# ScalarE's table loads moved to the end of the stages, and the masked attention's fill made by ScalarE

## The chip, the cores and the metric

The kernel runs on one core of a Trainium2 chip. A core has a matrix engine (TensorE, PE), a vector engine (VectorE, DVE), an activation engine (ScalarE, ACT), a general engine (GpSimd, POOL) and a queue for transfers (SyncE, SP). They run side by side, each in its own order, and wait for each other by semaphores. SBUF is the memory they work in, PSUM holds TensorE's results. The metric is device time in microseconds (us), lower is better. ScalarE looks its functions up in a table that holds one set of functions at a time; another set has to be loaded with an instruction of its own (ACT_TABLE_LOAD).

## The reference

Sixteen sequences of 128 tokens with 128 features pass through four layers, each with a cross attention and a feed-forward part, each part on a normalised copy of x and added to x through a gate:

```python
x = x + tanh(g_xattn[0]) * L0_xattn(layernorm(x), ctx, ...)     # correlation attention
x = x + tanh(g_ffn[0])   * L0_ffn(layernorm(x), ...)            # one of 8 experts
x = x + tanh(g_xattn[1]) * L1_xattn(layernorm(x), ctx, ...)     # 16 heads
x = x + tanh(g_ffn[1])   * L1_ffn(layernorm(x), ...)            # experts that choose tokens, silu
x = x + tanh(g_xattn[2]) * L2_xattn(layernorm(x), ctx, ...)     # 16 heads
x = x + tanh(g_ffn[2])   * L2_ffn(layernorm(x), ...)            # modulated MLP, gelu
x = x + tanh(g_xattn[3]) * L3_xattn(layernorm(x), ctx, mask, ...)
x = x + tanh(g_ffn[3])   * L3_ffn(layernorm(x), ...)            # small attention, 8 experts, gelu

def L3_xattn(q, k, v, mask, gamma, beta):                       # the masked attention
    logits = einsum('bsd,btd->bst', q, k) / sqrt(128)
    logits = where(mask == 0, -9e15, logits)
    x = einsum('bst,btd->bsd', softmax(logits), v)
    return layernorm_without_affine(x) * gamma + beta
```

All is float32, the mask is int32.

## The kernel before, in words

The whole model is one program. x stays in SBUF as X (128 tokens on the partitions, 16 x 128 columns), its normalised copy is XN, the transposed copy XNT. Each stage is one or several blocks. In a block every engine has its own list of instructions, and at its end all engines meet at a barrier. The order on each engine is the order in which the code is written; no scheduler changes it.

Stages in turn: input norm (L147), correlation attention (L197), experts 0, attention 1, experts 1 (L1350), attention 2, modulated MLP (L1407), masked attention (L1640), block attention (L1803), experts 3 (L2129).

`norm_pass` (L1372) is a block of its own that stands behind five of them: correlation, experts 0, experts 1, modulated MLP and masked attention. The stage has left the mean and variance of each token in `moments`. ScalarE loads the table set LOG_EXP (it has Ln, Exp and Copy), makes one over the square root of the variance out of Ln (L1384) and Exp (L1386), VectorE normalises 16 sequences (L1395), TensorE transposes them (L1403), and ScalarE copies the transposes to XNT (L1389). The experts of layers 1 and 3 go through `expert_quads`, whose ScalarE part (L1275) computes Silu or Gelu (L1285); the modulated MLP uses a tanh Gelu (L1600). Those functions need other table sets than LOG_EXP. The last block (L2149) normalises once more, with a table load of its own (L2152), Ln and Exp, ScalarE's scaling (L2159) and VectorE's sums (L2175 to L2187). LOG_EXP is also loaded at the start of the attentions (L886), of the masked attention (L1713) and of the block attention (L1924).

The masked attention works in four quarters q of four sequences (tiles of 128 x 512). GpSimd makes of the mask the tile hidden_key (1 where the mask is 0, L1673), fill (hidden_key times -9e15, L1676) and open_key (1 - hidden_key, L1677), with two buffers for the last two; behind q = 1 it adds the affine's second row to X, the residual base, in four operations (L1683), for which `scaled` (VectorE, L1790) must be there. TensorE makes the scores of all quarters (L1691), then for each quarter transposes the probabilities (L1699) and multiplies them with the context (L1707). VectorE's `softmax_rows(q)` scales and masks the scores (L1751), adds the fill (L1753), takes the maximum (L1754) and subtracts it (L1755, `shifted`); `output(q)` sums the probabilities (L1760), takes the reciprocal (L1761), scales the product (L1763) and takes its moments (L1765, L1768, `varied`); `add(q)` normalises it and adds it to X (L1777 to L1783), for which `based` must be there. VectorE's order is softmax 0, 1, output 0, softmax 2, output 1, softmax 3, add 0, output 2, add 1, output 3, add 2, add 3. ScalarE's order for each quarter is the exponential (L1718, `exped`), the copy of the transpose (L1722, `kept`), Ln and Exp for the output's norm (L1725, L1727). The functions that the diff touches:

## Time and profile before

| | |
|---|---|
| time before, median of 3 runs | 1493.91 us (1493.3 to 1495.25) |
| profiled execution | 1494.78 us, of it 1493.0 us in the span of the trace |
| TensorE busy | 1282.6 us, 86% |
| VectorE busy | 877.8 us, 59% |
| ScalarE busy | 711.9 us, 48% |
| GpSimd busy | 277.8 us, 19% |
| TensorE's granted clock, mean | 0.924 of full speed |
| the masked attention's block | 990.7 to 1037.4 us |

Times in the trace count from the start of the span. An instruction is busy from its start to its end; idle time of an engine is put down to what ended it. Where an engine is "released by PEq", "ACTq" or "issue", no work that the profile shows released it: it stood at a barrier or took up instructions. A granted clock of 1.00 is 2.4 GHz, of 0.50 it is 1.2 GHz.

### The profile page before, as it was taken

Reading aid. Unit: us, or ns where it says so; the run is one execution under the profiler, and the core shown is the slowest. Engines: PE = TensorE matmul, PEld = TensorE weight load, DVE = VectorE, ACT = ScalarE, POOL = GpSimd, SP = SyncE. Lnnn points to the kernel's source line nnn. Section 1 sums busy time; section 2 is a strip of 40 time slices with the busy share of each in tenths; the row PEclk is TensorE's granted clock in tenths of the full one; section 3 lists DMA queues with packets and bytes.
Section 4 is the critical chain, followed back from the end, with each engine's and each line's share of the span. In section 5 each row is a group of like instructions: output and inputs, shape, how many; then the busy total and the mean of one; then the engine's idle time right before and its main releaser. Section 6 shows DMA issues by size and latency. Waiting matters only on the chain. (4 is left out here: it accounts for less than half of the span.)

```text
span 1493.0 us, 26211 instructions
## 1 busy us (share of the span) xinstructions
PE 1282.6 (86%) x8587; PEld 958.4 (64%) x8587; DVE 877.8 (59%) x2280; ACT 711.9 (48%) x1529; POOL 277.8 (19%) x382
## 2 busy tenths in 40 slices
PE   6768489989987899779999979963999978999995
PEld 5742256666665487568888859852677764666664
DVE  4538788888873454556676643448687742222225
ACT  4323487777772302246666643432455533333333
POOL 1010032222231000023333330041443420000000
PEclk9869799999997999879999989965999978999998
DMA  9000000000000000000000022020000000000000
GB/s 349 2 1 0 1 1 1 2 1 2 2 1 1 1 1 0 1 1 2 2 2 2 2 59 70 1 113 1 1 2 0 0 1 0 0 1 1 0 1 29
DMA packets 6426, 24.48 MB, mean 16 GB/s; under 512 B 797, under 2 KB 1311, under 8 KB 5418
## 3 DMA queue, kind: packets, MB, share of 16 engines
q1 hardware_dynamic: 6314, 23.03, 4.5%
q8 instruction: 65, 1.06, 0.3%
q14 instruction: 47, 0.39, 0.1%
HBM read 21.98 MB, written 1.05 MB: 15 GB/s over the span
## 5 line engine op out<-in xcount | busy, mean ns | idle before, releaser
L1305 DVE SCALAR_TENSOR_TENSOR XN<-bank,gate,XN 128x128 f32<-128x128 f32 x256 | 89.9, 351 | 224.7 <-PE bank L1269 222.1
L1285 ACT ACTIVATE e_hidden<-bank,small 128x512 f32<-128x512 f32 x152 | 104.4, 687 | 214.8 <-PE bank L1257 214.7
L745 POOL TENSOR_TENSOR a_pn<-a_probs,a_rec 128x512 f32<-128x512 f32 x128 | 133.0, 1039 | 308.6 <-DVE a_rec L995 234.5
L1269 PEld LDWEIGHTS bank<-attention_weights,e_hidden 128*128 128x128 f32 x1024 | 119.2, 192 | 14.8 <-issue 14.8
L1009 DVE TENSOR_REDUCE a_mx<-bank 128x4 f32<-128x512 f32 x128 | 87.1, 681 | 70.2 <-PE bank L807 70.2
L1257 PE MATMUL bank<-XNT,attention_weights 128*128 128x512 f32 x256 | 121.2, 606 | 1.3 <-PEq L541 1.3
L1269 PE MATMUL bank<-attention_weights,e_hidden 128*128 128x128 f32 x1024 | 119.3, 275 | 0.0
L931 ACT ACTIVATE a_pT<-bank 128x512 f32<-128x512 f32 x128 | 76.1, 594 | 89.2 <-PE bank L842 89.0
L833 PE MATMUL bank<-attention_weights,a_cv 128*128 128x512 f32 x128 | 70.8, 635 | 27.3 <-issue 25.8
L1017 DVE TENSOR_TENSOR a_shifted<-bank,a_mx 128x512 f32<-128x512 f32 x128 | 88.3, 690 | 3.5
L990 DVE TENSOR_REDUCE a_total<-a_probs 128x4 f32<-128x512 f32 x128 | 86.5, 676 | 1.3 <-ACT a_probs L947 1.3
L1900 PEld LDWEIGHTS bank<-blk_va,blk_pT 128*128 128x128 f32 x512 | 64.3, 193 | 33.8 <-issue 21.8
L842 PEld LDWEIGHTS bank<-consts,a_pn 128*128 128x128 f32 x512 | 60.3, 141 | 38.0 <-issue 33.3
L947 ACT ACTIVATE a_probs<-a_shifted 128x512 f32<-128x512 f32 x128 | 80.0, 625 | 9.4 <-DVE a_shifted L1017 9.4
L1848 POOL TENSOR_TENSOR blk_kD<-blk_kT,consts 128x512 f32<-128x512 f32 x64 | 64.5, 1040 | 86.9 <-ACT blk_va L1947 86.9
L1257 PEld LDWEIGHTS bank<-XNT,attention_weights 128*128 128x128 f32 x256 | 40.8, 189 | 60.0 <-ACT e_hidden L1285 43.2
L842 PE MATMUL bank<-consts,a_pn 128*128 128x128 f32 x512 | 78.7, 276 | 0.8 <-ACT a_pT L931 0.7
L807 PE MATMUL bank<-a_kT,a_qT 64*128 64x128 f32 x1024 | 71.5, 279 | 0.6 <-DVE a_shifted L1017 0.6
L774 PE MATMUL bank<-a_pT,a_va 128*64 128x128 f32 x1024 | 70.0, 279 | 0.0
L807 PEld LDWEIGHTS bank<-a_kT,a_qT 64*128 64x128 f32 x1024 | 65.6, 189 | 6.9 <-issue 6.0
L1882 PE MATMUL bank<-blk_kD,blk_qT 128*128 128x512 f32 x128 | 67.9, 615 | 1.8 <-POOL blk_kD L1848 1.8
L821 PE MATMUL bank<-attention_weights,a_oT 128*128 128x128 f32 x512 | 65.7, 281 | 1.5 <-ACT a_oT L899 1.4
(351 smaller groups left out, 2584.9 us busy)
## 6 DMA issues: line engine op xcount, KB each, us to landing
attention_weights<-in_a SPq DMA_DIRECT2D x2, 2048.0 KB, 11.9
mod_ring<-in_mod_weights SPq DMA_DIRECT2D x4, 576.0 KB
ctx_both<-in_ctx SPq DMA_DIRECT2D x1, 2048.0 KB, 9.8
attention_weights<-in_up SPq DMA_DIRECT2D x1, 2048.0 KB, 7.9
attention_weights<-in_down SPq DMA_DIRECT2D x1, 2048.0 KB, 12.4
down<-in_down SPq DMA_DIRECT2D x1, 1536.0 KB, 18.3
down<-in_mod_weights SPq DMA_DIRECT2D x2, 576.0 KB
X<-in_x SPq DMA_DIRECT2D x4, 256.0 KB, 4.2
```

The costliest lines, as they stand in the source:

```text
L745: pool.tensor_tensor(pn[:, p, :].rearrange("p (h s) -> p h s", h=4), probs[:, p, :].rearrange("p (h s) -> p h s", h=4), rec[:, p, :].unsqu ...
L807: last = pe.matmul(score_bank[a][:, j * 128:(j + 1) * 128], qT[halves[a], p, at_pair:at_pair + 128], kT[halves[a], p, at_pair:at_pair + 12 ...
L842: last = pe.transpose(turn_bank[i.slot(turns)][:, j * 128:(j + 1) * 128], pn[:, p, j * 128:(j + 1) * 128], k.ident)
L931: act.activation(pT[:, i.slot(4), :], turn_bank[i.slot(turns)][:, :], ACT.Copy).then_inc(p_kept, 1)
L947: act.activation(probs[:, p, :], shifted[:, p, :], ACT.Exp, scale=W ** -0.5).then_inc(exped, 1)
L990: dve.tensor_reduce(total[:, p, :], probs[:, p, :].rearrange("p (h s) -> p h s", h=4), AX.X, ALU.add).then_inc(totalled, 1)
L1009: dve.tensor_reduce(mx[:, i.slot(2), :], score_bank[i.slot(2)][:, :].rearrange("p (h s) -> p h s", h=4), AX.X, ALU.max).then_inc(maxed, 1)
L1017: dve.tensor_tensor(shifted[:, p, :].rearrange("p (h s) -> p h s", h=4), score_bank[p][:, :].rearrange("p (h s) -> p h s", h=4), mx[:, p, ...
L1257: pe.matmul(bank[0:rows, :], up(g, f), col(k.XNT, q, 512), start=True, stop=True).then_inc(up_done, 1)
L1269: last = pe.matmul(down_bank[j][:, 0:width], layer[0:rows, f, j * 128:(j + 1) * 128], down(g, f), start=f == 0, stop=f == NB - 1)
L1285: act.activation(hidden[0:rows, p, f, :], up_bank_of(i, f)[0:rows, :], function, bias=up_bias(g, f)).then_inc(hidden_ready, 1)
L1305: dve.scalar_tensor_tensor(out=total, in0=down_bank[j][:, e * D:(e + 1) * D], scalar=gate_column(k, 4 * q + j, g * per_group + e), in1=tot ...
```

## The change

Five things change, all on ScalarE and GpSimd:
- the load of LOG_EXP at the head of `norm_pass`, of the last block, of the attentions, of the masked attention and of the block attention is taken out;
- it is added at the end of ScalarE's part of `expert_quads` (experts 1 and 3), behind the modulated MLP's last Gelu, and at the start of the correlation attention;
- in the masked attention hidden_key has two buffers, and `fill` is made by ScalarE (Copy with scale -9e15) instead of GpSimd: fills 0 and 1 ahead of all else, fill q + 2 behind the exponential of quarter q and ahead of the copy of its transpose;
- GpSimd adds the residual base behind all four masks instead of behind the second;
- VectorE's `softmax_rows` waits for `opened` and the new semaphore `filled`.

```diff
--- before.py
+++ after.py
@@ -272,6 +272,7 @@
 
             @block.scalar
             def _(act):
+                act.preload_act_table_set(LOG_EXP)
                 def body(at):
                     b = at(0)
                     if b.alive:
@@ -883,7 +884,6 @@
 
         @block.scalar
         def _(act):
-            act.preload_act_table_set(LOG_EXP)
 
             def square(i):
                 await_count(act, qk_projected, i.number + 1)
@@ -1286,6 +1286,7 @@
                                        bias=up_bias(g, f)).then_inc(hidden_ready, 1)
                 finish.scalar(act, batch_at(at))
             sweep(act, 4 * groups, groups, finish.depth * pace + FINISH, body)
+            act.preload_act_table_set(LOG_EXP)
 
         @block.vector
         def _(dve):
@@ -1380,7 +1381,6 @@
 
         @block.scalar
         def _(act):
-            act.preload_act_table_set(LOG_EXP)
             act.activation(moments[:, :, 1], moments[:, :, 1], ACT.Ln, bias=k.eps5[:, 0:1]).then_inc(logged, 1)
             act.wait_ge(logged, 1)
             act.activation(moments[:, :, 1], moments[:, :, 1], ACT.Exp, scale=-0.5).then_inc(rstd, 1)
@@ -1608,6 +1608,7 @@
                         keep_w2(n + 2)
                     if n + 1 < B:
                         gelu(n + 1)
+                act.preload_act_table_set(LOG_EXP)
 
             @block.vector
             def _(dve):
@@ -1645,11 +1646,12 @@
     with ExitStack() as ctx:
         sem = lambda what: nc.alloc_semaphore(f"single_{what}")
         sb = lambda what, shape, dt=F32: ctx.enter_context(nc.sbuf_tensor(f"single_{what}", shape, dt))
-        hidden_key, open_key, fill = sb("hidden_key", [128, 512]), sb("open_key", [128, 2, 512]), sb("fill", [128, 2, 512])
+        hidden_key, open_key, fill = sb("hidden_key", [128, 2, 512]), sb("open_key", [128, 2, 512]), sb("fill", [128, 2, 512])
         logits, probs, pT = sb("logits", [128, 2, 512]), sb("probs", [128, 2, 512]), sb("pT", [128, 2, 512])
         mx, rec = sb("mx", [128, 2, 4]), sb("rec", [128, 2, 4])
         o, stats, x_stats = sb("o", [128, 2, 512]), sb("stats", [128, 4, 6]), sb("x_stats", [128, B, 6])
         spread, moments = sb("spread", [128, 2, 4, 2]), sb("moments", [128, B, 2])
+        filled = sem("filled")
         marked, opened, scaled, based = sem("marked"), sem("opened"), sem("scaled"), sem("based")
         summed, x_summed, updated = sem("summed"), sem("x_summed"), sem("updated")
         scored, chain, shifted, exped = sem("scored"), sem("chain"), sem("shifted"), sem("exped")
@@ -1666,22 +1668,20 @@
             def _(pool):
                 pool.wait_ge(k.loaded["mask_ik1"], 16)
                 for q in range(4):
-                    if q:
-                        pool.wait_ge(opened, 2 * q)
                     if q >= 2:
+                        pool.wait_ge(opened, q - 1)
+                        pool.wait_ge(filled, q - 1)
                         pool.wait_ge(shifted, q - 1)
-                    pool.tensor_scalar(hidden_key[:, :], k.mask_ik1[:, q * 512:(q + 1) * 512], 0.0, None,
+                    pool.tensor_scalar(hidden_key[:, q % 2, :], k.mask_ik1[:, q * 512:(q + 1) * 512], 0.0, None,
                                        ALU.is_equal).then_inc(marked, 1)
                     pool.wait_ge(marked, q + 1)
-                    pool.tensor_scalar(fill[:, q % 2, :], hidden_key[:, :], NEG, None, ALU.mult).then_inc(opened, 1)
-                    pool.tensor_scalar(open_key[:, q % 2, :], hidden_key[:, :], -1.0, 1.0, ALU.mult,
+                    pool.tensor_scalar(open_key[:, q % 2, :], hidden_key[:, q % 2, :], -1.0, 1.0, ALU.mult,
                                        ALU.add).then_inc(opened, 1)
-                    if q == 1:
-                        pool.wait_ge(scaled, 1)
-                        for n in range(4):
-                            x = k.X[:, n * 512:(n + 1) * 512].rearrange("p (b d) -> p b d", b=4)
-                            pool.tensor_tensor(x, x, k.affine3(1).unsqueeze(1).to_broadcast([128, 4, D]),
-                                               ALU.add).then_inc(based, 1)
+                pool.wait_ge(scaled, 1)
+                for n in range(4):
+                    x = k.X[:, n * 512:(n + 1) * 512].rearrange("p (b d) -> p b d", b=4)
+                    pool.tensor_tensor(x, x, k.affine3(1).unsqueeze(1).to_broadcast([128, 4, D]),
+                                       ALU.add).then_inc(based, 1)
 
             @block.tensor
             def _(pe):
@@ -1710,12 +1710,21 @@
 
             @block.scalar
             def _(act):
-                act.preload_act_table_set(LOG_EXP)
+                def fill_hidden(q):
+                    act.wait_ge(marked, q + 1)
+                    if q >= 2:
+                        act.wait_ge(shifted, q - 1)
+                    act.activation(fill[:, q % 2, :], hidden_key[:, q % 2, :], ACT.Copy, scale=NEG).then_inc(filled, 1)
+
+                fill_hidden(0)
+                fill_hidden(1)
                 for q in range(4):
                     act.wait_ge(shifted, q + 1)
                     if q >= 2:
                         act.wait_ge(turned, q - 1)
                     act.activation(probs[:, q % 2, :], logits[:, q % 2, :], ACT.Exp).then_inc(exped, 1)
+                    if q + 2 < 4:
+                        fill_hidden(q + 2)
                     act.wait_ge(turned, q + 1)
                     if q >= 2:
                         act.wait_ge(weighted, q - 1)
@@ -1745,7 +1754,8 @@
                 def softmax_rows(q):
                     p, l = q % 2, logits[:, q % 2, :]
                     dve.wait_ge(scored, q + 1)
-                    dve.wait_ge(opened, 2 * q + 2)
+                    dve.wait_ge(opened, q + 1)
+                    dve.wait_ge(filled, q + 1)
                     if q >= 2:
                         dve.wait_ge(exped, q - 1)
                     link(dve.scalar_tensor_tensor(out=l, in0=k.ps[q][:, :], scalar=float(D) ** -0.5,
@@ -1921,7 +1931,6 @@
 
         @block.scalar
         def _(act):
-            act.preload_act_table_set(LOG_EXP)
 
             def body(at):
                 i = at(EXP)
@@ -2149,7 +2158,6 @@
         with nc.Block(no_gpsimd_drain=True) as block:
             @block.scalar
             def _(act):
-                act.preload_act_table_set(LOG_EXP)
                 v = moments[:, :, 1]
                 act.activation(v, v, ACT.Ln, bias=k.eps5[:, 1:2]).then_inc(logged, 1)
                 act.wait_ge(logged, 1)
```

How this stands on the engines. ScalarE at the end of the modulated MLP, the pass behind it and the head of the masked attention, the difference of before (-) and now (+); mod_u is the Gelu's output:

```order
 L1592 ACTIVATE mod_w<-bank 128x512
 L1600 ACTIVATE mod_u<-bank,mod_column_bias 128x128 x8
+L1611 ACT_TABLE_LOAD
 L1519 UNCONDITIONAL_BRANCH
-L1381 UNCONDITIONAL_BRANCH
-L1383 ACT_TABLE_LOAD
+L1382 UNCONDITIONAL_BRANCH
 L1384 ACTIVATE mod_moments<-mod_moments,eps 128x16
 L1386 ACTIVATE mod_moments<-mod_moments 128x16
 L1389 ACTIVATE XNT<-bank 128x512 x4
```

The load has moved from behind the barrier to ahead of it (the branches mark the ends and starts of blocks).

ScalarE in the masked attention's first two quarters now (before, it was L1713's load, then L1718, L1722, L1725, L1727 of each quarter in turn); single_probs is the exponential, single_pT the kept transpose:

```order
L1717 ACTIVATE single_fill<-single_hidden_key 128x512 x2
L1725 ACTIVATE single_probs<-single_logits 128x512
L1717 ACTIVATE single_fill<-single_hidden_key 128x512
L1731 ACTIVATE single_pT<-bank 128x512
L1734 ACTIVATE single_spread<-single_spread,eps 128x4
L1736 ACTIVATE single_spread<-single_spread 128x4
L1725 ACTIVATE single_probs<-single_logits 128x512
L1717 ACTIVATE single_fill<-single_hidden_key 128x512
L1731 ACTIVATE single_pT<-bank 128x512
```

Two fills stand ahead of the first exponential, and one each between an exponential and the kept transpose in the first two quarters.

GpSimd in the masked attention, before:

```order
L1673 TENSOR_SCALAR single_hidden_key<-mask_ik 128x512
L1676 TENSOR_SCALAR single_fill<-single_hidden_key 128x512
L1677 TENSOR_SCALAR single_open_key<-single_hidden_key 128x512
L1673 TENSOR_SCALAR single_hidden_key<-mask_ik 128x512
L1676 TENSOR_SCALAR single_fill<-single_hidden_key 128x512
L1677 TENSOR_SCALAR single_open_key<-single_hidden_key 128x512
L1683 TENSOR_TENSOR X<-X,affine 128x512 x4
L1673 TENSOR_SCALAR single_hidden_key<-mask_ik 128x512
L1676 TENSOR_SCALAR single_fill<-single_hidden_key 128x512
L1677 TENSOR_SCALAR single_open_key<-single_hidden_key 128x512
```

And now:

```order
L1675 TENSOR_SCALAR single_hidden_key<-mask_ik 128x512
L1678 TENSOR_SCALAR single_open_key<-single_hidden_key 128x512
L1675 TENSOR_SCALAR single_hidden_key<-mask_ik 128x512
L1678 TENSOR_SCALAR single_open_key<-single_hidden_key 128x512
L1675 TENSOR_SCALAR single_hidden_key<-mask_ik 128x512
L1678 TENSOR_SCALAR single_open_key<-single_hidden_key 128x512
L1675 TENSOR_SCALAR single_hidden_key<-mask_ik 128x512
L1678 TENSOR_SCALAR single_open_key<-single_hidden_key 128x512
L1683 TENSOR_TENSOR X<-X,affine 128x512 x4
```

Four operations have left GpSimd, and the four base adds have moved behind the third and fourth mask.

## Rows read from the trace of the kernel before

**Rows 1.** Groups: engine, tiles, count | busy us, mean ns | idle before, releasers.
```profile
L1383 ACT ACT_TABLE_LOAD x5 | 6.4, 1283 | 63.5 <-PEq L606 33.3 <-PEq L1220 15.8 <-PEq L1658 7.0
...
L1718 ACT ACTIVATE single_probs<-single_logits 128x512 f32<-128x512 f32 x4 | 2.5, 617 | 5.7 <-DVE single_logits L1755 5.7
```
**Rows 2.** Timeline, pass behind experts 0: start, duration, engine, line, idle before.
```profile
159.50 0.36 DVE L473 BATCH_NORM_AGGREGATE e_moments<-e_stats 128x2 f32<-128x6 f32 x4
160.19 1.28 ACT L1383 ACT_TABLE_LOAD   x1 [33.34 <-PEq L606]
161.48 0.31 ACT L1384 ACTIVATE e_moments<-e_moments,eps 128x16 f32<-128x16 f32 x1
...
162.07 4.19 DVE L1395 TENSOR_SCALAR XN<-X,e_moments 128x128 f32<-128x128 f32 x16 [2.22 <-ACT e_moments L1386]
```
**Rows 3.** Timeline, ScalarE at the modulated MLP's end.
```profile
975.76 2.17 ACT L1600 ACTIVATE mod_u<-bank,mod_column_bias 128x128 f32<-128x128 f32 x8
...
981.73 1.28 ACT L1383 ACT_TABLE_LOAD   x1 [3.80 <-PEq L1519]
```
**Rows 4.** Timeline, ScalarE's first work in correlation and in block attention.
```profile
16.93 0.60 ACT L282 ACTIVATE cor_fqk<-bank 128x512 f32<-128x512 f32 x1 [4.26 <-PE bank L247]
...
1046.51 0.28 ACT L1945 ACTIVATE blk_qT<-bank 128x128 f32<-128x128 f32 x1 [0.27 <-PE bank L1874]
```
**Rows 5.** Timeline, the last block.
```profile
1480.47 1.28 ACT L2152 ACT_TABLE_LOAD   x1 [11.06 <-PEq L1220]
...
1481.04 0.69 DVE L2175 TENSOR_TENSOR X<-X,affine 128x512 f32<-128x512 f32 x1
...
1482.36 0.17 DVE L2179 SCALAR_TENSOR_TENSOR last_shrunk<-last_moments 128x16 f32<-128x16 f32 x1 [0.62 <-ACT last_moments L2156]
```
**Rows 6.** Timeline, the masked attention.
```profile
990.71 6.57 PE L1691 MATMUL bank<-ctx_both,XNT 128*128 128x128 f32 x32 [2.38 <-PEq L2254]
...
990.80 1.57 POOL L1673 TENSOR_SCALAR single_hidden_key<-mask_ik 128x512 f32<-128x512 int32 x1 [101.08 <-POOLq L2254]
...
992.45 1.49 POOL L1676 TENSOR_SCALAR single_fill<-single_hidden_key 128x512 f32<-128x512 f32 x1
994.02 0.62 POOL L1677 TENSOR_SCALAR single_open_key<-single_hidden_key 128x512 f32<-128x512 f32 x1
...
994.76 0.69 DVE L1751 SCALAR_TENSOR_TENSOR single_logits<-bank,single_open_key 128x512 f32<-128x512 f32 x1 [3.21 <-POOL single_open_key L1677]
...
998.34 0.66 PE L1699 MATMUL bank<-consts,single_probs 128*128 128x128 f32 x4 [1.06 <-ACT single_probs L1718]
998.46 5.83 POOL L1683 TENSOR_TENSOR X<-X,affine 128x512 f32<-128x512 f32 x4
...
999.33 0.94 DVE L1753 TENSOR_TENSOR single_logits<-single_logits,single_fill 128x512 f32<-128x512 f32 x1
...
999.68 1.89 PE L1707 MATMUL bank<-ctx_both,single_pT 128*128 128x128 f32 x8 [0.69 <-ACT single_pT L1722]
...
1002.79 0.69 DVE L1763 TENSOR_TENSOR single_o<-bank,single_rec 128x512 f32<-128x512 f32 x1
...
1005.14 0.61 ACT L1718 ACTIVATE single_probs<-single_logits 128x512 f32<-128x512 f32 x1
...
1007.61 2.07 PE L1707 MATMUL bank<-ctx_both,single_pT 128*128 128x128 f32 x8 [0.69 <-ACT single_pT L1722]
...
1008.11 0.69 DVE L1751 SCALAR_TENSOR_TENSOR single_logits<-bank,single_open_key 128x512 f32<-128x512 f32 x1 [3.44 <-issue]
...
1011.81 0.69 DVE L1763 TENSOR_TENSOR single_o<-bank,single_rec 128x512 f32<-128x512 f32 x1
...
1013.61 0.66 DVE L1751 SCALAR_TENSOR_TENSOR single_logits<-bank,single_open_key 128x512 f32<-128x512 f32 x1
```
**Rows 7.** Waits, 988 to 1040: who for whom, us in total, times, longest.
```profile
DVE single_logits L1751 <- POOL single_open_key L1677: 4.2, 2, 3.2
```
**Rows 8.** Window: length, busy of PE, PEld, DVE, ACT, POOL, PEclk, DMA, GB/s.
```profile
639.00:651.00 12.00, 9.54 (x40) 8.24 (x42) 2.73 (x4) 3.60 (x5) 1.41 (x6) 0.50 0.00 0
```

## The prediction

> **What bounds the kernel now.** I read the page first: the span is 1493.0 us, TensorE is busy in most of it, and ScalarE, VectorE and GpSimd have room. But the program is a row of blocks with a barrier behind each, so a share of the span says nothing about a short block: there the engine that ends last decides, and every microsecond in front of the barrier is a microsecond of the kernel. The chain of waits covers only the final block for that reason. So I read next the groups of ScalarE's instructions (where does it load a table, and what stood idle before it), then the timeline around one load of each kind, and last the timeline of the masked attention.
>
> In the groups the pass's load (L1383) stands five times at 1283 ns, each with idle time before it [rows 1]. The timeline of one pass shows the bound. VectorE's last moments end at 159.86 (159.50 + 0.36), the load starts at 160.19, the logarithm at 161.48, and VectorE, idle for 2.22, starts normalising at 162.07 when ScalarE's exponential is done [rows 2]. Nothing else works meanwhile: load, logarithm and exponential are the path.
>
> The masked attention (990.7 to 1037.4) looks different. GpSimd makes three tiles for each quarter of the mask in 1.57, 1.49 and 0.62, and VectorE can't begin before 994.76; it waits for GpSimd twice, 4.2 us together, 3.2 and so 1.0 [rows 6, 7]. Then GpSimd adds the base to X for 5.83 us ahead of the third mask, and VectorE waits again, 3.44 us, until 1008.11 [rows 6]. (The view puts that wait down to "issue"; the mask operations behind the base adds fill exactly this time: 998.46 + 5.83 + 1.49 + 1.49 + 0.62 and some gaps is 1008.0.) From 1013.61 on VectorE runs through, so whatever comes earlier at that point ends the block earlier.
>
> **The five passes.** Each loses its load between barrier and logarithm: 161.48 - 160.19 = 1.29 [rows 2], times five [rows 1] = 6.45. What is late next is logarithm and exponential, 0.59, still ahead of VectorE: it enters its block with the other engines, so it won't be later than they are. What hides the load at its new place:
> - behind the modulated MLP's last GELU, which ends at 977.93 (975.76 + 2.17): ScalarE is idle 3.80 until the barrier [rows 3], the load takes 1.28. This is the tightest; without that cover it would cost the 1.28 again.
> - behind the two expert stages ScalarE is idle 15.8 and 11.06 [rows 1, 5].
> - at the start of the correlation ScalarE waits 4.26 for TensorE [rows 4].
> - the passes behind correlation, experts 0 and masked attention need no load, since only Copy, Exp and Ln run on ScalarE in between.
>
> The other loads that vanish (both attentions, masked attention, block attention) give nothing: ScalarE still waits for a product behind them, 0.27 in the tightest [rows 4]. Cost and gain 0.
>
> **The last block.** The logarithm comes 1.29 earlier there too, but VectorE isn't idle: it works on X until 1481.73 (1481.04 + 0.69) and only then would take up the shift that it makes now at 1482.36 [rows 5]. So that shift starts at about 1481.76, and everything behind it, ScalarE's normalising and the output, moves by 0.60. Sum of the tables: 6.45 + 0.60 = 7.05.
>
> The Trainium skill speaks against so small a price. Its page "ScalarE: Activation LUTs", section "What ACT_TABLE_LOAD costs", gives 1283 ns for the load and some 1380 ns for a drain, 2.66 us for every switch to another set. The trace has the same 1283 ns, but no drain: the logarithm starts 0.01 behind the load. By that page of the Trainium skill the five passes would bring some 13 us (an estimate, 5 x 2.66), by the rows 6.45; the sum goes by the rows.
>
> **The masked attention.** ScalarE's fill is a Copy of 128x512 from SBUF to SBUF; its exponential of that form takes 617 ns [rows 1], so I take 0.62. Step by step, on the times of before:
> - GpSimd: key 0 until 992.37, then at once the open key, until 993.07; ScalarE fills from 992.4 to 993.0 beside it. VectorE starts at 993.19 instead of 994.76: 1.57 earlier. Its four operations for a quarter take 2.88 (0.69 each and 0.03 between, as from the row at 994.76 on): done 996.07.
> - GpSimd: key 1 until 994.64, open until 995.35, fill 1 at 995.3: VectorE goes on without a wait, 996.07 to 998.95.
> - The exponential is done at 996.7, but TensorE is in its scores until 997.28 (990.71 + 6.57), then transposes for 0.66: 997.95. ScalarE has fill 2 queued ahead of keeping that transpose. Key 2 waits for VectorE's 996.07, so it ends at 997.6, fill 2 at 998.27, the copy of the transpose at 998.9 (0.3 later than without fill 2), and the products run from 998.95 for 1.89: 1000.85. They began at 999.68 before, so only 0.73 of the 1.57 is kept here, and VectorE, which has meanwhile done its sum, now waits 1 us for TensorE. Part of these products would now fall under the higher clock; I take VectorE's scaling at 1000.8 instead of 1002.79: 2.0 earlier.
> - From there the order before gives the distances: exponential 1 starts 2.35 behind that scaling (1005.14 - 1002.79), its products 2.47 later and take 2.07. So 1003.15, 1005.6, 1007.7, and the second scaling starts at 1007.8 instead of 1011.81: 4.0 earlier. Of the 2.47, 1.2 is neither exponential nor copy but TensorE's transposes; fill 3 (0.62) lies in it and costs nothing.
> - Is VectorE ready by then? It starts the third quarter at 1002.7 (mask 2 is long made, the 3.44 wait is gone), reaches its scaling 3.70 later (1011.81 - 1008.11, where it had no wait), and up to 0.5 more because the base adds now run beside it: the fill's addition took 0.94 beside them, two such additions and subtractions lie in a quarter [rows 6]. That is 1006.9, so it waits 0.9, and this contention is hidden.
> - Base adds: mask 3 is done at 1001.2, they run to 1007.1. The first that needs them is the update of X, which VectorE makes behind its fourth quarter of logits, and that quarter only starts at 1009.6. Hidden.
> - The fourth quarter starts 1.80 behind the second scaling (1013.61 - 1011.81), 4.0 earlier, and so does all behind it.
>
> Least for this part: the 1.57 at the start and nothing of the rest. Most: all three waits gone and no new one, 1.57 + 1.0 + 3.44 = 6.0. I take 4.0, what the chain by rows gives.
>
> As to the contention, "SBUF — State Buffer", section "SBUF: two separate sides", of the Trainium skill says that VectorE with two SBUF inputs and GpSimd exclude each other for a whole instruction. The row shows 0.25 more and no full wait; by this page of the Trainium skill, as an estimate, it might be a microsecond more per addition, most of it under the 0.8 wait.
>
> **Sum.** 7.05 + 4.0 = 11.05. The profiled execution has span 1493.0 and a time of 1494.78, 1.8 around it that the change doesn't touch; the median of the runs is 1493.91, 0.9 lower. I take the 11.05 off both: span about 1481.9, time 1493.91 - 11.05 = **1482.9**.
>
> **Rivals.**
> - *The masked attention only wins its start.* TensorE and ScalarE in turn become its bound: fill 2 ahead of the kept transpose, scores ahead of the transposes. For it: 0.84 of the first 1.57 is lost there at once. Against it: the 3.44 wait has nothing to do with that chain. Gain 7.05 + 1.57: 1485.3.
> - *No new wait at all.* The products come under the higher clock. 7.05 + 6.0: 1480.9. Against it: the scores of 6.57 stand in the way.
> - *More than the load goes.* Part of the 0.33 between VectorE's end and the load might be ScalarE's own, not the barrier's. At most 5 x 0.33 = 1.7 more: 1481.2. Against it: nothing else starts sooner either. The drain that the Trainium skill's page on ScalarE names would be this, and larger.
> - *The loads leave the passes, but not the path:* VectorE isn't ready sooner, say because its block is entered late. Then only 4.0 remains: 1489.9. Against it: it is idle 2.22 and released by the exponential.
> - *Slower: TensorE enters stages at 1.2 instead of 2.4 GHz.* All stages start at other moments than before. In the second attention's first 12 us the granted clock is 0.50 with TensorE busy for 9.54 [rows 8]; at 2.4 GHz this work would take about half, so such a start costs up to 4.8. If three more stages started like that, 14.3 would go and the time is 1493.91 - 11.05 + 14.3 = 1497.2. It decides from 11.05, over two such starts. For it: clocks do differ from start to start. Against it: idle time of TensorE ahead of each start gets shorter, not longer, and each step of the change only shortens it.
>
> **How the numbers follow.** My case 0.70, masked start only 0.12, no new wait 0.05, more than the load 0.05, passes give nothing 0.04, slower 0.04. The range reaches from 1479.0 (no new wait and the 0.33s) to 1487.5 (masked start only, with half of a slow start, 2.4, on top). About 0.2% (3 us) is what a measurement can tell from no change. All cases but the last lie more than that below 1493.91; slow starts in between would land within it: faster 0.95, same 0.02, slower 0.03.
>
> **What would show it.** In each pass the logarithm 0.3 behind VectorE's last moments, no table load between, and VectorE idle 0.9. A load at the end of both expert stages and of the modulated MLP with idle time behind it. In the last block 0.60. In the masked attention VectorE's first product 2.5 behind the block's start instead of 4.1, no wait for GpSimd, two waits for TensorE of 0.8 to 1.1, and the block 4.0 shorter. I am wrong if the block shrinks by 2 or less, if a pass keeps more than 0.3 of its 1.29, or if long stages between change by more than 2 us.

## The result, and the profile after

| | before | after |
|---|---|---|
| median, us | 1493.61 (1491.88 to 1495.25, 4 runs) | 1478.89 (1476.86 to 1479.45, 4 runs) |
| ratio | | 0.9899, 95% interval 0.9882 to 0.9916 |
| the same comparison again | 1493.66 (16 runs) | 1477.9 (4 runs), 0.9896, 0.9881 to 0.9911 |
| profiled execution: time, span | 1494.78, 1493.0 | 1478.38, 1476.6 |
| ScalarE's table loads | 15 | 9 |
| mean granted clock | 0.924 | 0.929 |

The kernel is faster, as forecast, but by 15 to 16 us instead of 11. The median lies 0.1 below the stated range. All eight runs of the changed kernel together have a median of 1478.3; that is the base for the single changes below. Kernels were measured in sets, each with runs of before beside it; against the 1493.66 of before in the same two sets it is 15.4 faster. So there are some 4 us to find.

The pass behind the correlation, ScalarE and VectorE from the timeline of the changed kernel (start, duration, engine, line, operation, tiles, idle time before and what ended it):

```profile
81.48 0.36 DVE L474 BATCH_NORM_AGGREGATE cor_moments<-cor_stats 128x2 f32<-128x6 f32 x4
82.19 0.31 ACT L1384 ACTIVATE cor_moments<-cor_moments,eps 128x16 f32<-128x16 f32 x1 [3.54 <-PEq L378]
82.53 0.22 ACT L1386 ACTIVATE cor_moments<-cor_moments 128x16 f32<-128x16 f32 x1
82.78 4.19 DVE L1395 TENSOR_SCALAR XN<-X,cor_moments 128x128 f32<-128x128 f32 x16 [0.94 <-ACT cor_moments L1386]
```

The logarithm starts 0.35 behind VectorE's last moments (81.48 + 0.36 to 82.19), where the load stood before [rows 2]; VectorE is idle for 0.94 instead of 2.22. The other four passes look the same (0.94 to 0.96 instead of 2.22 to 2.24). The loads at their new places, from the groups of ScalarE's instructions:

```profile
L1289 ACT ACT_TABLE_LOAD x2 | 2.6, 1283 | 0.0
...
L275 ACT ACT_TABLE_LOAD x1 | 1.3, 1283 | 0.3 <-PEq L150 0.3
...
L1611 ACT ACT_TABLE_LOAD x1 | 1.3, 1283 | 0.0
```

They cost 1283 ns as before, but with idle time behind them: 2.09 behind the modulated MLP's.

The masked attention, from the timeline of the changed kernel, to be read beside [rows 6]:

```profile
979.39 6.22 PE L1691 MATMUL bank<-ctx_both,XNT 128*128 128x128 f32 x32 [2.38 <-PEq L2262]
...
981.08 0.63 ACT L1717 ACTIVATE single_fill<-single_hidden_key 128x512 f32<-128x512 f32 x1 [3.43 <-POOL single_hidden_key L1675]
981.13 0.62 POOL L1678 TENSOR_SCALAR single_open_key<-single_hidden_key 128x512 f32<-128x512 f32 x1
...
981.85 0.69 DVE L1761 SCALAR_TENSOR_TENSOR single_logits<-bank,single_open_key 128x512 f32<-128x512 f32 x1 [1.62 <-POOL single_open_key L1678]
...
986.42 0.63 ACT L1717 ACTIVATE single_fill<-single_hidden_key 128x512 f32<-128x512 f32 x1 [1.04 <-POOL single_hidden_key L1675]
...
986.96 0.58 ACT L1731 ACTIVATE single_pT<-bank 128x512 f32<-128x512 f32 x1
...
987.59 1.16 PE L1707 MATMUL bank<-ctx_both,single_pT 128*128 128x128 f32 x8 [1.50 <-ACT single_pT L1731]
...
988.86 0.69 DVE L1773 TENSOR_TENSOR single_o<-bank,single_rec 128x512 f32<-128x512 f32 x1 [0.42 <-PE bank L1707]
...
989.96 5.85 POOL L1683 TENSOR_TENSOR X<-X,affine 128x512 f32<-128x512 f32 x4
...
991.39 1.62 DVE L1763 TENSOR_TENSOR single_logits<-single_logits,single_fill 128x512 f32<-128x512 f32 x1
...
995.86 0.69 DVE L1773 TENSOR_TENSOR single_o<-bank,single_rec 128x512 f32<-128x512 f32 x1 [0.37 <-PE bank L1707]
...
997.67 0.69 DVE L1761 SCALAR_TENSOR_TENSOR single_logits<-bank,single_open_key 128x512 f32<-128x512 f32 x1
```

Counted from VectorE's first instruction in the block (990.72 before, 979.40 now), its first product stands at 2.45 instead of 4.04, the second scaling at 16.46 instead of 21.09, the fourth quarter at 18.27 instead of 22.89. That is 4.6, where 4.0 was forecast. The first products ran at 2.4 GHz (1.16 for eight, granted clock 1.00), where the sum had 1.89.

Then the timeline has a difference that no step of the prediction has. The router behind the correlation's pass, in the groups of TensorE's instructions (84 to 100 us), before:

```profile
L489 PE MATMUL bank<-small,XNT 128*128 128x8 f32 x32 | 7.0, 361 | 1.0 <-PEq L1375 1.0
L1403 PE MATMUL bank<-consts,XN 128*128 128x128 f32 x16 | 4.3, 464 | 4.6 <-DVE XN L1395 4.6
```

and after:

```profile
L490 PE MATMUL bank<-small,XNT 128*128 128x8 f32 x32 | 5.3, 308 | 1.0 <-PEq L1376 1.0
```

The same 32 instructions take 1.7 less. Windows of the changed kernel show why (length, then busy time of PE, PEld, DVE, ACT, POOL, then TensorE's granted clock, DMA's share and GB/s):

```profile
84.00:87.00 3.00, 3.00 (x13) 2.09 (x12) 2.98 (x12) 1.68 (x3) 0.00 (x0) 0.54 0.00 0
88.00:91.00 3.00, 2.66 (x21) 2.69 (x21) 0.00 (x0) 0.00 (x0) 2.60 (x3) 0.86 0.00 0
91.00:94.00 3.00, 2.66 (x13) 2.56 (x13) 0.29 (x1) 0.00 (x0) 1.43 (x2) 0.50 0.00 0
```

and of the kernel before:

```profile
91.00:95.00 4.00, 3.89 (x19) 3.92 (x19) 0.00 (x0) 0.00 (x0) 3.83 (x4) 0.50 0.00 0
95.00:98.00 3.00, 3.00 (x15) 2.98 (x14) 0.00 (x0) 0.00 (x0) 0.20 (x1) 0.50 0.00 0
```

Now the clock is at 2.4 GHz for the router's first part; before it was at 1.2 GHz for all of it.

To see where else time went I use the starts of VectorE's normalising in the five passes and of the last block's shift (L2179 before), from each kernel's timeline. The intervals between them, in us (each holds the gap of the pass at its end):

| kernel | over experts 0 | attention 1, experts 1 | attention 2, MLP | masked attention | block attention, experts 3 |
|---|---|---|---|---|---|
| before | 76.67 | 467.15 | 354.40 | 55.68 | 443.06 |
| after | 73.20 | 464.22 | 352.09 | 49.84 | 443.84 |
| after, again | 73.37 | 464.55 | 350.70 | 49.83 | 442.38 |

By the forecast the first three get shorter by 1.29 each. They got shorter by 3.4, 2.8 and 3.0. TensorE's busy time in the first and the third of these intervals, before:

```profile
85.40:162.07 76.67, 48.92 (x121) 23.30 (x121) 52.90 (x194) 21.48 (x107) 7.17 (x12) 0.79 0.00 0
...
629.22:983.62 354.40, 331.69 (x2902) 282.76 (x2902) 204.52 (x448) 191.40 (x400) 86.54 (x117) 0.94 0.06 15
```

and after:

```profile
82.78:155.98 73.20, 46.72 (x121) 21.36 (x121) 52.90 (x194) 20.18 (x106) 7.17 (x12) 0.83 0.00 1
...
620.20:972.29 352.09, 330.22 (x2902) 282.53 (x2902) 204.49 (x447) 190.08 (x399) 86.56 (x117) 0.95 0.06 15
```

The same 121 matmuls take 2.2 less, the same 2902 take 1.5 less (2.9 less in the second run of the changed kernel, at 0.96). In the interval over attention 1 the busy time hardly changes (407.50, then 407.26 and 406.91), so its excess is not seen there.

### The profile page after: what moved, and what is told of

Same layout as the page of the kernel before. It is cut to its first block and busy times, and to the rows that moved or that the text cites. A ratio compares the mean times of both kernels' runs of the same rounds, so it can differ in the third digit from the quotient of the medians.

```text
span 1476.6 us, 26209 instructions
## 1 busy us (share of the span) xinstructions
PE 1277.3 (87%) x8587; PEld 955.2 (65%) x8587; DVE 878.3 (59%) x2280; ACT 706.0 (48%) x1527; POOL 271.8 (18%) x378
## 5 line engine op out<-in xcount | busy, mean ns | idle before, releaser
L1910 PE MATMUL bank<-blk_va,blk_pT 128*128 128x9 f32 x512 | 65.7, 256 | 2.0 <-ACT blk_pT L1978 1.6
```

The lines of the kernel that those rows point to most:

```text
L1910: last = pe.matmul(value_bank[p][:, h * (W + 1):(h + 1) * (W + 1)], pT[:, i.slot(2), j * 128:(j + 1) * 128], va[:, p, h, :], start=True, s ...
```

## The experiments

My theory A: the shorter gap in a pass (the stretch between VectorE's last moments and its normalising, in which TensorE has nothing to do) changes when TensorE's clock stands at 2.4 GHz in the stages behind it, and this brings what the rows of loads don't show. Rival B: the tables bring what the rows say, and the rest is the masked attention or scatter. Rival C: a load costs more than its duration.

**The two halves of the change apart.** Tables alone: the masked attention is that of before, with no load of its own.

> The moved table loads alone; the masked attention is that of before (GpSimd makes the fill, base adds behind the second mask), without its load. Theory A (the excess over the forecast comes from TensorE's clock at stage entries, which the shorter gaps change): the rows' 7.05 plus some 3, so 9 to 11 us faster than before, with a mean granted clock above before's 0.924. Theory B (the rows were complete for the tables, the excess is the masked attention's or noise): 7.0 plus or minus 1. Theory C (each removed load also had a hidden drain of about 1.4): 13 to 14 us faster, and the gap between VectorE's last moments and the logarithm below 0.33.

Masked attention alone:

```diff
 def stage_masked_attention(nc, k):      # as in the changed kernel, all else as before
             def _(act):
+                act.preload_act_table_set(LOG_EXP)
                 def fill_hidden(q):
```

> The masked attention of the changed kernel alone (ScalarE's fill, base adds last), all table loads where they were before. By the changed kernel's trace the block is 4.6 shorter. Theory A: 4.6 plus or minus 1 faster, since only the entry of one stage moves. Theory B: 4.6 plus the excess of 3, 7 to 8. In its trace the block's VectorE part takes 41.8 instead of 46.35.

Measured: tables alone 1483.53, ratio 0.9935 (0.9922 to 0.9949), 10.1 faster; masked attention alone 1489.6, 0.9973 (0.9962 to 0.9984), 4.1 faster. Its block's interval is 51.05 instead of 55.68, so 4.6. The excess is the tables': 10.1 against 7.05, with an interval that leaves 7.05 out. Rival B falls. The two halves add up to 14.2, 1.2 less than both together; the scatter of the medians allows that.

**The time of the load put back without a load**, in all five passes:

```diff
         def _(act):                                         # norm_pass
+            act.activation(k.XNT[:, 0:1400], k.X[:, 0:1400], ACT.Copy)
             act.activation(moments[:, :, 1], ...Ln...)
```

> The changed kernel with a copy of 128x1400 on ScalarE (about 1.3 us) ahead of the logarithm in each of the five passes: the time of the load is put back, without a load. If only the path's length counts, it is 6.4 slower than the changed kernel (rows alone) or some 9 slower (if the longer gaps also cost clock at the entries, theory A). If the load itself has a cost beyond its duration (theory C), it stays below 7.

> The changed kernel once more, to place it among the others of this set and to see how time and mean granted clock go together from run to run. All theories: 14.7 plus or minus 1.5 faster than before. Theory A: the runs with the higher mean clock are the faster ones, some 0.5 us for 0.001.

ScalarE's timeline of the kernel with the copy:

```profile
82.26 1.37 ACT L1385 ACTIVATE XNT<-X 128x1400 f32<-128x1400 f32 x1 [3.54 <-PEq L378]
83.53 0.29 ACT L1386 ACTIVATE cor_moments<-cor_moments,eps 128x16 f32<-128x16 f32 x1
```

Each logarithm is 1.27 later, 6.35 in all, but the kernel takes 1490.06 (0.9975 of before, 0.9966 to 0.9985): 11.75 above the changed kernel's 1478.3, more than the 9 that theory A had. Its first interval is 76.33, the router takes 6.96 again. No table was loaded there, and taking a load out of a pass had shortened its gap by no more than the load's own 1.28, so rival C falls: the longer gap costs almost twice its time, with a copy in it as with a load.

The changed kernel once more took 1477.9, 15.8 below before, as expected. Its eight runs are in the order of the mean clock: the three with 0.933 took 1476.9 to 1477.6, the four with 0.929 took 1478.4 to 1479.5, so some 0.5 us for 0.001, as expected too. Among the 45 runs of before in the sets of the experiments, the 13 with 0.922 or less took 1494.5 and more, the 32 others 1491.6 to 1495.2.

**TensorE kept busy in the gap**, in before with 5 and in the changed kernel with 3 matmuls:

```diff
         def _(pe):                                          # norm_pass
+            for _ in range(5):
+                pe.matmul(k.ps[7][:, 0:128], k.ident, k.ident, start=True, stop=True)
             for q in range(B // 4):
```

> The kernel before with five matmuls on constants, into a bank nobody reads, on TensorE at the start of each of the five passes, beside the table load and the logarithm (VectorE isn't ready before, so no wait gets longer). Theory A (the excess of 3 to 5 us is TensorE's clock at the stages behind the passes): 3 to 6 us faster than before, higher mean granted clock, and the pass behind correlation to the pass behind experts 0 takes about 73.3 plus 1.3 instead of 76.6. Theory B (the excess has another cause): within 1 of before, or up to 1 slower.

> The changed kernel with three such matmuls at the start of each pass, in the shorter gap. Theory A: the changed kernel has most of this gain already, so 0 to 3 us faster than it. Theory B: no change, or up to 1 slower where the third matmul runs past VectorE's first tile.

Measured: 1492.62, 0.9990 of before (0.9981 to 0.9999), and 1477.27, 0.9885 (0.9869 to 0.9900). In before this is 1.5, below the 3 us that theory A had, and the first interval hardly moved (76.54 instead of 76.67). The matmuls ran (the rows are of before with them), the mean clock rose from 0.924 to 0.930, but the clock was down again for the transposes and the router:

```profile
82.00:85.00 3.00, 1.35 (x10) 1.19 (x10) 0.83 (x7) 1.79 (x3) 0.00 (x0) 0.92 0.03 8
85.00:90.00 5.00, 4.32 (x16) 2.91 (x16) 4.19 (x16) 2.00 (x5) 0.00 (x0) 0.50 0.00 0
90.00:98.00 8.00, 6.96 (x32) 6.90 (x32) 0.24 (x1) 0.41 (x1) 4.03 (x4) 0.50 0.00 0
```

So theory A needs mending: these five matmuls in the gap didn't raise the clock for the router. What is left to set it is when the pass's transposes and the router come, and the copies in single passes below try that. Part of what the matmuls did raise lay where TensorE waits for others: in the interval of the masked attention the mean clock is 0.63 instead of 0.53, and its length 55.56 instead of 55.68.

**Order and entry loads.** Fills 2 and 3 behind the kept transpose (the two calls exchanged), and the four priced loads put back:

> The changed kernel with ScalarE's fills 2 and 3 behind the kept transpose instead of ahead of it. The prediction priced fill 2's place at 0.3 on the first products. If that is right the masked attention gets 0.2 to 0.4 shorter, unless fill 3 then comes in VectorE's way; the time changes by less than a measurement can tell.

> The changed kernel with the table loads put back at the start of both attentions, the masked attention and the block attention, four loads of 1.28. The prediction priced them at nothing, as ScalarE waits for TensorE there: the same time within 1. If they cost (a rival cause of the excess: a load at an entry delays the stage), it is 2 to 5 us slower.

Measured: 1478.27 (ratio 0.9894, 0.9879 to 0.9909), the block's interval 49.43 instead of 49.84, and 1478.56 (0.9899, 0.9884 to 0.9914). Both as expected: fill 2's place costs 0.4, the loads at the stages' entries nothing. The row of the first products, with the fills behind, shows what the 0.4 hides:

```profile
987.55 1.16 PE L1707 MATMUL bank<-ctx_both,single_pT 128*128 128x128 f32 x8 [0.69 <-ACT single_pT L1729]
```

The block starts at 980.17 there, so the products start 7.38 behind it instead of 8.19 (987.59 - 979.40). Fill 2's place delays them by 0.8, where the prediction had 0.3; VectorE, then without a wait, keeps all but 0.4 of it.

**The copy in one pass at a time**, then half of it in the first:

```diff
+            if name == "cor":                               # "e0", "e1", "mod", "single"
+                act.activation(k.XNT[:, 0:1400], k.X[:, 0:1400], ACT.Copy)     # half: 620 columns
```

> The changed kernel with the 1.27 us copy ahead of the logarithm in one pass only, the one behind the correlation. Theory A, as the stage intervals of the first eight kernels have it (normalising to normalising over experts 0 is 76.5 with the long gap and 73.2 with the short one, of which 1.3 is the pass itself): this one gap costs 1.27 + 1.9 at once, the router's matmuls take 6.96 again instead of about 5.2, and the time is 3 us or more above the changed kernel. If the extra cost needs all gaps together: 1.3 only.

> The same with half the copy, some 0.6 us. Theory A with a step (the clock changes at once or not at all): the router's matmuls take either about 5.3 or 6.96, nothing between. A gradual effect would give some 6.1.

> The changed kernel with the copy in the pass behind experts 1 only. The interval from there over the second attention to the modulated MLP's pass was 354 with long gaps and 350.7 to 352.2 with short ones. Theory A: the shift of 1.27 brings it back to about 353 to 354 through the clock at the modulated MLP's entry, 2 to 3 us above the changed kernel. If that stage's excess is only scatter: 1.3 above.

> The changed kernel with the 1.27 us copy in the pass behind experts 0 only. Theory A (a longer gap can also cost clock at what comes next, here attention 1 and experts 1; the interval over them was 467 with long gaps and 464.2 to 466.9 with short ones): 2 to 4 above the changed kernel. Without such a cost: 1.3.

> The copy in the pass behind the modulated MLP only, ahead of the masked attention, whose first 6 us of scores run at 1.2 GHz anyway: 1.3 to 2 above the changed kernel by theory A, 1.3 without a cost of the clock.

> The copy in the pass behind the masked attention only, ahead of the block attention and experts 3. The interval over them was 442.4 to 445.1 in all kernels with no order by the gap: 1.3, plus or minus 1. If the sum of the five single copies is to reach 11.7, the three of this set have to bring about 6.6 together.

| copy in the pass behind | median, us | above 1478.3 | beyond 1.27 |
|---|---|---|---|
| correlation | 1481.9 | 3.6 | 2.3 |
| experts 0 | 1480.4 | 2.1 | 0.8 |
| experts 1 | 1479.84 | 1.5 | 0.3 |
| modulated MLP | 1479.93 | 1.6 | 0.4 |
| masked attention | 1478.72 | 0.4 | -0.9 |
| all five | 1490.06 | 11.75 | 5.4 |

The medians are of four runs each (ten for all five) that scatter by about 1, so only the correlation's row and that of all five stand clear of it. The sets differ as well: before's median was 1493.36 with the copies behind correlation and experts 1, 1494.59 with the other three, 1493.66 with all five. Taken against before of their own set, the single copies cost 3.9, 1.2, 1.8, 0.7 and -0.5 in the table's order, 7.1 in sum. Theory A had 2 to 4 behind experts 0, 2 to 3 behind experts 1, and 6.6 for the last set's three copies together, which brought 4.1: these expectations weren't met, or only just.

The trace with the copy behind the correlation names the place: the interval over experts 0 is 75.04, though the copy lies ahead of it, against 73.2 to 73.4. With half the copy there is one run only, 1479.02, from which no cost of 2 can be read; its profile has the interval over experts 0 at 75.51. From TensorE's groups:

```profile
L490 PE MATMUL bank<-small,XNT 128*128 128x8 f32 x32 | 7.0, 361 | 1.0 <-PEq L1376 1.0
L1405 PE MATMUL bank<-consts,XN 128*128 128x128 f32 x16 | 4.3, 464 | 3.9 <-DVE XN L1397 3.9
```

and of the changed kernel's second run:

```profile
L490 PE MATMUL bank<-small,XNT 128*128 128x8 f32 x32 | 4.8, 291 | 1.0 <-PEq L1376 1.0
L1403 PE MATMUL bank<-consts,XN 128*128 128x128 f32 x16 | 4.3, 437 | 3.3 <-DVE XN L1395 3.3
```

It is a step. Transposes 3.3 behind TensorE's last products: the router at 4.7 to 5.5 in all twelve profiles of that kind, two of them with matmuls in between. Transposes 3.9 or 4.6 behind: 6.96 in all six of that kind, one of them with matmuls in between. In the profiles half the delay costs the router's stage the same 2. The last products before the pass start anywhere from 77.8 to 80.3 in these profiles, with no effect on which of the two kinds it is, so what decides is the distance within the kernel, not the moment of the run.

The copy behind experts 1 showed its own excess in its profile (the interval over attention 2 and the MLP is 353.09), but that was its slowest run, 1481.82; the other three are at 1479.0 to 1480.0. I don't take it as shown.

**A version further:** no open_key, the scores scaled and the fill added in one VectorE operation.

```diff
                     ...                                     # GpSimd's open_key and the waits for it are gone too
                     link(dve.scalar_tensor_tensor(out=l, in0=k.ps[q][:, :], scalar=float(D) ** -0.5,
-                                                  in1=open_key[:, p, :], op0=ALU.mult, op1=ALU.mult))
-                    link(dve.tensor_tensor(l, l, fill[:, p, :], ALU.add))
+                                                  in1=fill[:, p, :], op0=ALU.mult, op1=ALU.add))
```

> A version further: the changed kernel without open_key. The scores are scaled and the fill added in one VectorE operation, since -9e15 plus a logit is -9e15 in float32. VectorE loses four operations of 0.72 and, in the third quarter, the addition that took 1.62 beside the base adds; GpSimd loses four of 0.62. Part of it turns into waits for TensorE (0.4 were there already): the masked attention's block 2 to 3 shorter than 41.8, the time 2 to 3 below the changed kernel.

> The version without open_key, with three matmuls on constants on TensorE at the start of each pass as well. Without open_key was 1.0 below the changed kernel, the matmuls alone 1.0; together 1 to 2 below the changed kernel, 1476 to 1477.5, if the two gains are separate.

Measured: 1477.32, 0.9891 of before (0.9875 to 0.9908), and with the matmuls in the passes 1477.24, 0.9883 (0.9866 to 0.9899). Both lie below the changed kernel's 1478.3 by 1.0, within the scatter of the medians, so better than it by timing isn't shown; the matmuls add nothing. The block's interval is 48.26 instead of 49.83: 1.6, where 2 to 3 was expected. The timeline without open_key says where the rest went:

```profile
988.85 0.69 DVE L1767 TENSOR_TENSOR single_o<-bank,single_rec 128x512 f32<-128x512 f32 x1 [1.26 <-PE bank L1703]
...
990.65 0.66 DVE L1756 SCALAR_TENSOR_TENSOR single_logits<-bank,single_fill 128x512 f32<-128x512 f32 x1
...
992.06 1.82 DVE L1759 TENSOR_TENSOR single_logits<-single_logits,single_mx 128x512 f32<-128x512 f32 x1
...
995.86 0.69 DVE L1767 TENSOR_TENSOR single_o<-bank,single_rec 128x512 f32<-128x512 f32 x1 [1.17 <-PE bank L1703]
```

VectorE has less to do and waits 1.26 and 1.17 for TensorE's products, instead of 0.42 and 0.37: there the chain over ScalarE and TensorE bounds the block. The block starts at 980.17 there, so the first scaling comes at 8.68 instead of 9.46 and the second at 15.69 instead of 16.46. The operation saved in the first quarter brings 0.8, as the first exponential comes earlier; those of the second and third quarter only lengthen VectorE's waits; the one of the fourth, where VectorE no longer waits, brings the other 0.8. And the long operation beside the base adds is now the subtraction.

## Why the prediction was right or wrong, point by point

- **The five passes, 6.45: right.** Each lost 1.28, seen by VectorE's idle time (2.22 to 0.94), and the copies put 1.26 back there (2.20). The covers held, ScalarE had 2.09 to spare behind the modulated MLP's load.
- **The last block, 0.60: nearly right.** From the block's first ScalarE instruction to its normalising it was 2.10 and is 1.36 (1464.81 to 1466.17), 0.74: VectorE took up the shift at 1465.97, before its operation on X had fully ended.
- **Loads at the entries, 0: right**, shown by putting them back.
- **The masked attention, 4.0: the term was undersized, 4.6.** The mechanism held: first product 1.6 earlier, no wait for a third mask, two new waits for TensorE. The 0.6 is all there at the first scaling, 2.6 earlier where I took 2.0; behind it the distances were as forecast (exponential 2.35, products 2.47 later). I took the first products at nearly 1.89, they took 1.16, as they fell under the higher clock. I had this only in the case without any new wait (0.05), and the waits did come, 0.42 and 0.37 instead of 0.8 to 1.1. The products started where I had them, 8.19 behind the block's start (8.23 forecast), with fill 2 in the way; only its price was off, 0.8 instead of 0.3, since the transposes were ready 0.5 earlier than I had them. The contention was much larger than the 0.5 I allowed, 1.62 instead of 0.69 for one addition and 0.92 for the subtraction, and it was hidden as forecast, since VectorE waited for TensorE behind it.
- **The step that failed is the bound on the clock.** "Idle time of TensorE ahead of each start gets shorter, not longer, and each step of the change only shortens it" stood there as an argument against the slower case alone. I let the clock of the stages behind the passes take time away, never give it back, and so the sum had no term for it and the lower end of the range none either. The runs put about 4 us in its place. Of these 2 are shown: the gap behind the correlation, transposes 3.9 or more behind the last products against 3.3, decides over 1.5 to 2.3 in the router. Another 1.7 is the excess of the third interval, over attention 2 and the modulated MLP; there TensorE's busy time fell by 1.5 to 2.9 for the same matmuls and its mean clock rose from 0.94 to 0.95 and 0.96, but no single gap was shown to do it. The 1.5 over attention 1 stays open: the busy time didn't fall there, and the interval also takes two values from profile to profile (464.2 to 464.6 or 466.4 to 467.0 in kernels with the short gap at its end). Each of these is from one or two profiled executions, and 2.1, 1.5 and 1.7 come to more than the 3.6 that the medians leave. Nor is it shown that the effects of the gaps add up: the single copies cost 7.1 to 9.2 in sum, all five 11.75. The prediction's own sign, a long stage between that changes by more than 2, was there: the stretch over experts 0 got shorter by 3.4, of which its pass is 1.3.
- **The sum.** 7.05 + 4.0 was forecast. With 4.6 and 0.74 it is 11.8; 15.4 was measured (1493.66 and 1478.3). Of the 3.6 left, 2 are shown to be the clock's in the router, the rest isn't shown to be. The lower end of the range, by its own terms (no new wait and the 0.33s), is 1479.2 and not 1479.0.
- The rival "more than the load goes" wasn't it: the gap between VectorE's end and the logarithm is still 0.35. Two of the five loads changed the set (behind experts 1 and the modulated MLP), three repeated the active one; all five gave 1.28, so the prediction's 5 x 2.66 counted changes of set that weren't there, and the two real ones showed no drain either.

## What to carry to other kernels

A table load right behind a barrier, with nothing else at work, cost its full time here, 1.28. Put it behind the last use of the old set, where the engine idles, and look for the next instruction on the path to see how much of it counts: all in the passes, 0.7 in the last block, nothing at the stages' entries. Price a shortened gap for TensorE too: if a burst of matmuls follows it at 1.2 GHz, look at the granted clock there in windows, and give the sum a term, or at least the range a bound, for its coming earlier on the faster side, in a step and not in proportion. A higher mean clock is not a gain by itself: look whether TensorE is what the others wait for there.

## What the runs showed of the hardware

- A delay of 0.6 us on ScalarE cost 0.6 in its pass and, in its one profile, another 2.1 to 2.3 in the stage behind it, where the router's matmuls fell back from between 4.7 and 5.5 us to 6.96. This split held in all profiled executions, twelve with the short gap and six with a longer one.
- GpSimd's additions and VectorE's, both with two inputs in SBUF: an addition of VectorE's took 1.62 and, without open_key, a subtraction 1.82 instead of 0.69; others took 0.92 beside them. The Trainium skill, page "SBUF — State Buffer", section "SBUF: two separate sides", has the loser wait for the whole instruction of the other. The 0.93 and 1.13 more agree with a wait of up to one base add, which takes 1.46 or, without open_key, 1.23 (5.85 and 4.93 for four); that the 0.25 which the prediction went by [rows 6] was a case with little of the other left isn't shown. With the fills behind the kept transpose the same addition took 0.77, so one row doesn't give the price: it depends on how the two meet.
- Five matmuls in each gap raised the mean granted clock from 0.924 to 0.930 and brought 1.5 us; the changed kernel has 0.929 and is 15 faster. Between two kernels mean clock and time are not to be read for each other, though the runs of one kernel follow it.
